# Delta-rule output read out with tokens on partitions, the root of the mean square applied at the residual

## The reference

```python
# log_alpha <= 0 per key channel, Gg its running sum within a chunk; M lower triangular, from keys, decays, beta
u = solve_triangular(M, vg - kexp @ S)                 # unit diagonal
o = SCALE * ((qg * exp(Gg)) @ S + attn @ u)            # attn: decayed products of query and keys
S = exp(glast) * S + kdec.T @ u
...
rstd = rsqrt(mean(square(o), axis=-1) + NORM_EPS)      # over the 128 value channels
o = o * rstd * onorm_w * sigmoid(gate)
x = x + o.reshape(b, t, H * DV) @ Wo.T
```

## Time and profile before

| | us |
|---|---|
| median of three runs | 5018.0 |
| span of the profiled execution | 5005.7 |
| VectorE busy | 4134.4 (83%) |
| ScalarE busy | 3484.7 (70%) |
| GpSimd busy | 3217.8 (64%) |
| mean of 60 periods, 428.26 to 4621.15 | 69.88 |

### The profile page before, as it was taken

The page is one execution under the profiler, slowest core; times in us unless marked ns, Lnnn a source line. Parts: engine busy times, 40 slices in busy tenths (PEclk is TensorE's granted clock), DMA queues, the critical chain, the costliest instruction groups (busy, mean ns, idle before and its releaser), DMA issues.

```text
span 5005.7 us, 151432 instructions
## 1 busy us (share of the span) xinstructions
PE 4517.9 (90%) x63200; PEld 3131.9 (63%) x63200; DVE 4134.4 (83%) x7262; ACT 3484.7 (70%) x6775; POOL 3217.8 (64%) x5316
## 2 busy tenths in 40 slices
PE   8869999999999999999999999899999999999888
PEld 5536666666666666666666666666666666666655
DVE  3289998888988899889998899888998899988622
ACT  3367777777777777777777777777777777777531
POOL 0047777776777777777777777777777777777600
PEclk9979999999999999999999999999999999999899
DMA  2200000000000000000100000000000000000100
GB/s 88 94 21 21 25 25 25 16 22 25 34 32 15 28 25 25 25 14 25 34 32 28 15 25 25 25 16 23 30 29 25 14 24 25 25 25 8 38 9 21
DMA packets 49724, 135.45 MB, mean 27 GB/s; under 512 B 7056, under 2 KB 28176, under 8 KB 48400
## 3 DMA queue, kind: packets, MB, share of 16 engines
q1 hardware_dynamic: 49040, 125.77, 7.2%
HBM read 111.60 MB, written 14.16 MB: 25 GB/s over the span
## 4 chain that ended last, share of the span: by engine, by line
PE 54%; DVE 26%; ACT 11%; issue 7%; POOL 1%; DMA 0%; DVEq 0%; SPq 0%; ACTq 0%
PE bank L835 46%; DVE acc L1557 8%; PE bank L302 7%; DVE X L1554 7%; DVE sp_t L1554 2%; ACT L1432 2%; DVE Pd L1662 2%; ACT Us L1181 2%; ACT o L1182 1%; DVE Zc L1741 1%; DVE Rs L1557 1%; DVE o L1557 1%; ACT acc L1181 1%; PE bank L906 1%; DVE x1m L1554 1%
## 5 line engine op out<-in xcount | busy, mean ns | idle before, releaser
L1557 DVE SCALAR_TENSOR_TENSOR acc<-bank,vc,acc 128x510 f32<-128x510 f32 (+2 forms) x1728 | 1272.9, 740 | 148.5 <-ACT acc L1181 122.9
L2002 POOL TENSOR_TENSOR LZ<-LZ,LT 128x120 f32<-128x120 f32 (+26 forms) x1984 | 957.3, 483 | 155.5
L1999 POOL TENSOR_TENSOR LT<-LA,LZ 128x120 f32<-128x120 f32 (+26 forms) x1984 | 917.1, 462 | 145.9
L1554 DVE TENSOR_TENSOR X<-KQ,Fl 128x640 f32<-128x640 f32 x1024 | 1002.8, 995 | 1.5 <-ACT Fl L1182 1.5
L1972 POOL COPY X<-KQ 128x640 f32<-128x640 f32 x256 | 246.4, 962 | 912.4 <-PE bank L835 312.2
L835 PE MATMUL bank<-X 128*32 128x60 f32 (+1 forms) x32768 | 650.8, 205 | 132.6 <-DVE Pd L1662 85.9
L835 PEld LDWEIGHTS bank<-X 128*32 128x32 f32 x32768 | 524.7, 112 | 369.1 <-issue 211.0
L1181 ACT ACTIVATE Us<-bank 128x128 f32<-128x128 f32 x1024 | 281.2, 276 | 621.3 <-PE bank L835 615.2
L835 PE MATMUL bank<-xnTm,WK 128*128 128x512 f32 x1280 | 662.7, 643 | 42.0 <-DVE acc L1557 36.3
L835 PE MATMUL bank<-Rs,Ztf 128*128 128x128 f32 x2048 | 467.4, 314 | 68.8 <-DVE Rs L1557 48.6
L1951 POOL TENSOR_TENSOR kdec<-KQ,Fe 128x512 f32<-128x512 f32 x256 | 336.8, 1316 | 299.4 <-PE bank L906 299.4
(11 more groups left out here) (145 smaller groups left out, 9346.4 us busy)
## 6 DMA issues: line engine op xcount, KB each, us to landing
WK<-in_wkq SPq DMA_DIRECT2D x64, 704.0 KB, 5.9
WV<-in_wv SPq DMA_DIRECT2D x64, 576.0 KB, 3.8
WO<-in_wo SPq DMA_DIRECT2D x64, 128.0 KB, 2.0
wuh<-in_wu SPq DMA_DIRECT2D x2, 1024.0 KB, 7.4
xt<-in_x SPq DMA_DIRECT2D x4, 512.0 KB, 6.2
wuh_d<-wuh SPq DMA_DIRECT2D x1, 2048.0 KB, 6.3
x_d<-x SPq DMA_DIRECT2D x4, 512.0 KB, 3.1
xnT_d<-xT SPq DMA_DIRECT2D x4, 512.0 KB, 2.7
```

The source lines that it names most:

```text
L1554: return e.tensor_tensor(o, a, b, op)
L1557: return e.scalar_tensor_tensor(out=o, in0=a, scalar=sc, in1=b, op0=op0, op1=op1)
L1999: e.tensor_tensor(tmp, LA[:, j + 1:32, 8 * (j % R) + j // R].unsqueeze(2).broadcast_to([P, rr, cc]), LZ[:, j, 0:cc].unsqueeze(1).broadcast ...
L2002: e.tensor_tensor(LZ[:, j + 1:32, 0:cc], LZ[:, j + 1:32, 0:cc], tmp, SUB).then_inc(g_row, 1)
```

## The change

Four things are changed together.

1. The output is computed with tokens on partitions. `update` keeps only the product for S (chunk 7 has none). A new `attend(s, j)`, j = 0 to 3, computes the outputs of chunks 2j and 2j + 1 of both sequences: At and qn are now the weights (32 columns) and Us and S move (128 columns); each chunk writes 32 partitions of bank 7. Us and S get four buffers per sequence. attend(0) stands behind update(1, 1), attend(1) behind update(1, 4), attend(2) behind update(1, 6), attend(3) behind project_k(p, 4), which goes ahead of it.
2. The mean square is a sum along the free axis: ScalarE copies bank 7 to o2, and squares bank 7 in four parts with `accum_out`, onto itself. Ln and Exp work on four columns (`rstd`). The matmul with ones is gone. `keep(p-1, 0)` goes ahead of the squares.
3. TensorE turns o2 back by four transposes (`turn_o`, behind products(p-1, 1, 0)); VectorE multiplies by the gate alone; the weight onorm_w is multiplied into WO on GpSimd (`weigh_out`); `rstd` is applied where VectorE adds to x1, in four parts. A block of tokens on partitions is 64 tokens of each sequence, so x1 is loaded and stored by two DMAs each.
4. LB and x1 have one buffer each.

The order in bank_use becomes ... v 1, k 3, k 4, oturn 0, out 0, out 1, gate 0 ... .

```diff
-            ("ms", 0, 3, a_ms, 3, 0), ("k", 4, 0, v_ck, 15, 14), ("out", 0, 3, v_out, 2, 0),
-            ("out", 1, 3, v_out, 2, 1), ("gate", 0, 1, a_gate, 1, 0), ("vturn", 0, 2, a_vt, 4, 0),
+            ("k", 4, 0, v_ck, 15, 14), ("oturn", 0, 3, v_o, 1, 0), ("out", 0, 3, v_out, 4, 1),
+            ("out", 1, 3, v_out, 4, 3), ("gate", 0, 1, a_gate, 1, 0), ("vturn", 0, 2, a_vt, 4, 0),
...
 TensorE
-                if c < 7:
-                    mm(bank[5 + hb][:, 2 * P:3 * P], kdT[:, s % 2, u, :], Us[:, hb, :]).then_inc(p_upd, 1)
-                o = bank[7][:, 32 * u:32 * u + 32]
-                ins = mm(o, Us[:, hb, :], At[:, s % 2, u, :], True, c == 0)
-                if c:
-                    ins = mm(o, S[:, hb, c % 2, :], qn[:, s % 2, 32 * u:32 * u + 32], False, True)
+                mm(bank[5 + hb][:, 2 * P:3 * P], kdT[:, s % 2, 8 * hb + c, :], Us[:, hb, c % 4, :]).then_inc(p_upd, 1)
+
+            def attend(s, j):
+                w.wait_ge(a_ssq, every(s - 1, 4))
+                w.wait_ge(a_Us, nth(s, 16, 4 * j + 3))
+                chunks = [(hb, c) for hb in range(2) for c in (2 * j, 2 * j + 1)]
+                for hb, c in chunks:
+                    o = bank[7][half(2 * hb + c % 2), P * j:P * j + P]
+                    ins = mm(o, At[:, s % 2, 8 * hb + c, :], Us[:, hb, c % 4, :], True, c == 0)
+                for hb, c in chunks:
+                    o = bank[7][half(2 * hb + c % 2), P * j:P * j + P]
+                    u = 8 * hb + c
+                    if c:
+                        ins = mm(o, qn[:, s % 2, 32 * u:32 * u + 32], S[:, hb, c % 4, :], False, True)
                 ins.then_inc(p_o, 1)
...
-            def mean_square(s):
-                o = bank_for("ms", 0, s)
-                w.wait_ge(a_osq, every(s, 1))
-                mm(o[:, :], ones, o2[:, :]).then_inc(p_ms, 1)
+            def turn_o(s):
+                o = bank_for("oturn", 0, s)
+                w.wait_ge(a_o, every(s, 1))
+                for j in range(4):
+                    ins = e.transpose(o[:, P * j:P * j + P], o2[:, P * j:P * j + P], ident)
+                ins.then_inc(p_ot, 1)
...
                 solve(p - 3, 1, 7)
                 spare(p - 3, 22)
-                update(p - 3, 0, 7)
-                update(p - 3, 1, 7)
+                project_k(p, 4)
+                attend(p - 3, 3)
                 spare(p - 3, 23)
-                mean_square(p - 3)
-                project_k(p, 4)
                 products(p - 1, 1, 0)
+                turn_o(p - 3)
 ScalarE
                 w.wait_ge(p_sol, nth(s, 16, 2 * c + hb))
-                act(Us[:, hb, :], bank[5 + hb][:, P:2 * P], ACT.Copy).then_inc(a_Us, 1)
+                w.wait_ge(p_o, nth(s - 1, 4, c // 2 + 2) if c < 4 else nth(s, 4, c // 2 - 2))
+                act(Us[:, hb, c % 4, :], bank[5 + hb][:, P:2 * P], ACT.Copy).then_inc(a_Us, 1)
...
-                act(o2[:, :], bank[7][:, :], ACT.Square, scale=SCALE).then_inc(a_osq, 1)
+                act(o2[:, :], bank[7][:, :], ACT.Copy).then_inc(a_o, 1)
+            def out_square(s, j):
+                o = bank[7][:, P * j:P * j + P]
+                e.activation(o, o, ACT.Square, scale=SCALE, accum_out=ssq[:, j:j + 1]).then_inc(a_ssq, 1)
...
-                out_square(p - 3)
+                out_copy(p - 3)
                 e.preload_act_table_set("natural_log_exp_and_others")
                 decay(p, 2)
+                keep(p - 1, 0)
+                out_square(p - 3, 0)
...
                 out_root(p - 3, 0)
                 out_root(p - 3, 1)
-                keep(p - 1, 0)
                 tap_k(p, 4)
 VectorE
-                    stt(o2[:, :], sg[:, s % 2, :], 1.0, o2[:, :], ADD, MUL).then_inc(v_o, 1)
-                    stt(o2[:, :], bank[7][:, :], hon[:, 0:1], o2[:, :], MUL, MUL).then_inc(v_o, 1)
+                for b in range(2):
+                    ins = stt(ov[:, b], gv[:, b], 1.0, tv[:, b], ADD, MUL)
...
-                tt(xv, bank[bank_use["out", q, s][0]][:, :], xv, ADD).then_inc(v_out, 1)
+                b = bank[bank_use["out", j // 2, s][0]][:, D * (j % 2):D * (j % 2) + D]
+                stt(x1[:, j, :], b, rstd[:, j:j + 1], x1[:, j, :], MUL, ADD).then_inc(v_out, 1)
...
                 evacuate(p - 1, 1, 0)
                 output(p - 3, 0)
+                output(p - 3, 1)
                 evacuate(p - 1, 1, 1)
                 evacuate(p - 1, 1, 2)
-                output(p - 3, 1)
+                output(p - 3, 2)
+                output(p - 3, 3)
                 evacuate(p - 1, 1, 3)
 GpSimd, behind level(p - 1, 2)
+                e.tensor_scalar(WO[:, s % 2, :], WO[:, s % 2, :], hon[:, 0:1], None, MUL).then_inc(g_wo, 1)
 SyncE
-                w.wait_ge(g_row, every((n - 1) * H - 1, 62))
+                w.wait_ge(v_Cn, every(n * H - 1, 2))
...
-                w.wait_ge(d_x2[n % 2], 16 * (n // 2))
-                e.dma_start(x1[:, n % 2], by_tile(x1_d)[n]).then_inc(d_x1[n % 2], 16)
+                if n:
+                    w.wait_ge(d_x2[(n - 1) % 2], 32 * ((n + 1) // 2))
+                for hb in range(2):
+                    e.dma_start(x1[64 * hb:64 * hb + 64], by_chunk(x1_d)[n, hb]).then_inc(d_x1, 16)
```

More of the change, by code:

```diff
@@ L660, in build @@
         onw = vc[:, H * 39:H * 39 + 1]
[L661 removed]
+        x1 = sb("x1m", [P, 4, D])
         tctx.close()
@@ L674, in build @@
         p_inv = [sem(f"p_inv{i}") for i in range(4)]
-        p_rhs, p_sol, p_upd, p_o, p_ms, p_out = (sem(f"p_{n}") for n in ("rhs", "sol", "upd", "o", "ms", "out"))
+        p_rhs, p_sol, p_upd, p_o, p_ot, p_out = (sem(f"p_{n}") for n in ("rhs", "sol", "upd", "o", "ot", "out"))
         a_tapk, a_tapv, a_k, a_v, a_gate, a_decay = (sem(f"a_{n}") for n in ("tapk", "tapv", "k", "v", "gate", "decay"))
@@ L686, in build @@
         v_Rs, v_S, v_o, v_out = (sem(f"v_{n}") for n in ("Rs", "S", "o", "out"))
-        g_zero, g_kdec, g_kexp, g_copy, g_X0, g_init, g_row = (sem(f"g_{n}") for n in ("zero", "kdec", "kexp", "copy", "X0", "init", "row"))
+        g_zero, g_kdec, g_kexp, g_copy, g_X0, g_init, g_row, g_wo = (sem(f"g_{n}") for n in ("zero", "kdec", "kexp", "copy", "X0", "init", "row", "wo"))
         def turns(order, count):
@@ L791, in delta_sync @@
                     if h == H - 1:
[L792 to L795, removed]
+                        store_x1(n)
+                        if n + 1 < NT:
+                            load_x1(n + 1)
                 s = p - 1
@@ L1068, in delta_tensor @@
                 update(p - 3, 1, 4)
+                attend(p - 3, 1)
                 spare(p - 3, 14)
@@ L1086, in delta_tensor @@
                 update(p - 3, 1, 6)
+                attend(p - 3, 2)
                 spare(p - 3, 20)
@@ L1159, in delta_tensor @@
                 update(p - 2, 1, 1)
+                attend(p - 2, 0)
                 spare(p - 2, 5)
@@ L1324, in turned @@
                 if q == 0:
-                    w.wait_ge(p_o, every(s - 2, 16))
+                    w.wait_ge(p_upd, every(s - 2, 14))
                 act(kdT[:, s % 2, 4 * q:4 * q + 4, :].rearrange("p n d -> p (n d)"),
@@ L1332, in keep @@
                 w.wait_ge(p_prod, nth(s, 20, 5 * b + 4))
-                w.wait_ge(p_o, every(s - 2, 16))
+                w.wait_ge(p_o, every(s - 2, 4))
                 w.wait_ge(v_bd, every(s - 2, 1))
@@ L1345, in place @@
                 w.wait_ge(v_Ztc, every(s, 1))
-                w.wait_ge(p_o, every(s - 1, 16))
+                w.wait_ge(p_sol, every(s - 1, 16))
                 act(Ztf[q, :, q], Ztc[q, :, :], ACT.Copy).then_inc(a_Ztf, 1)
@@ L1960, in spread @@
                 else:
-                    w.wait_ge(p_o, every(s - 2, 16))
+                    w.wait_ge(p_rhs, every(s - 2, 14))
                     scaled(kexp[:, s % 2, 4 * q:4 * q + 4], Fe[:, 0, :]).then_inc(g_kexp, 1)
```

112 lines of the change are left out of this document (66 added, 46 removed).

## The result

The changed kernel takes 5299.4 us (median of four runs, 5296.75 to 5301.17) where the kernel before took 5016.3 in the same comparison: a ratio of 1.056, with a 95% interval of 1.0539 to 1.0577. The direction was as forecast (0.75 for slower), the size was not: +283 us where +116 was forecast, outside the range of 4985 to 5210.

The account below looks back on a forecast made before the run. No engine bounds the whole: VectorE bounds unfold to beta step, recurrence and read-out are chains between engines. Read-out +3.6 us less recurrence gain 1.7 gives +1.9 a period, 115 us in 60: 5134 us, range 4985 to 5210.

Parts of the forecast that it names:

- The read-out chain: From TensorE's last chunk to the unfold: project_k(p, 4) ahead and ScalarE's later copy lengthen it by 3.6 us a period.
- TensorE's wait (near 3 us): Sign of being right: TensorE's wait behind the last attend is its longest, near 3 us, put down to ScalarE's E.
- output(0) waiting for acc: Sign of being right, in the read-out: output(0) waits for VectorE's acc, since it uses the bank of key block 4.
- How much of the 3.0 arrives? ... Taken: 1.7: Recurrence: of TensorE's 3.0 us of saved work a period, 1.7 shortens the path; bounds 0.8 and 3.0.
- shrinks by 1.2 to 2: Sign of being right: the time from beta step to last convolution of v shrinks by 1.2 to 2 us.
- I leave the clock's cost ... as it is: Clock term, whole period: its cost stays 0.94 us a period, despite a longer stand-still of 3.1 us.
- a fall in every period, twice: Rival: clock falls in two stretches every period, costing 2.7 us for 0.94: 5238 us; 0.15 for beyond the forecast.
- part of the slow work lies in slack: Argument against the clock rival: some work at the lower clock lies in slack; no size given.
- Buffers 0: Single buffers for beta and x1: three changes of tile at 0 us each, 5 at most.
- The tiling rule as a rival: Rival, recurrence: TensorE's saving wins, read-out keeps its length, 1.77 us a period gained, 4912 us; chance 0.17.

Follow-up runs that it names:

- e2: Changed kernel plus 14 unused TensorE matmuls behind attend(3), filling its 3.3 us wait: 5216.4 us, ratio 1.040 to the kernel before.
- e6: Changed kernel with e5's read-out order, and attend(0), (1), (2) moved to where TensorE waits anyway: 4906.0 us, ratio 0.978 to the kernel before.
- e5: Changed kernel with read-out reordered: attend(3), turn_o, project_k(p, 4); banks in that order; ScalarE's block 4 tap before squares and roots: 4998.7 us, ratio 0.9967 to before.
- e8: Kernel before plus unused fill matmuls, three ahead of mean_square and two behind it: 5032.4 us, ratio 1.004.
- e4: Kernel before with one buffer each for beta and x1, nothing else of the change: 5019.8 us against 5022.4, ratio 1.0004.
- e7: Changed kernel with only its three early attend groups moved to e6's places, read-out unchanged: 5275.5 us, ratio 1.051 to the kernel before.
- e10: Changed kernel with attend(0), (1), (2) cut to one matmul each, other outputs of chunks 0 to 5 left out: 5274.0 us, ratio 1.051 to before.

## Why the prediction was right in direction and wrong in size

**The read-out chain: right, 0.5 us short.** Counted from the start of `project_k(p, 4)`, forecast against e2 at full clock and against after:

| us from project_k(p, 4) | forecast | e2, full clock | after |
|---|---|---|---|
| copy of o | 2.4 | 2.6 | 2.6 |
| tap of block 4 | 7.1 | 7.4 | 7.4 |
| gating | 6.7 | 7.1 | 8.0 |
| output(0) | 10.1 | 10.5 | 11.1 |
| unfold | 13.4 | 13.95 | 14.9 |

Squares and roots took 1.26 and 0.44 (2530.46 to 2531.72 to 2532.16) for 1.1 and 0.5; the attend group 0.58 for 0.5 to 0.6; no table was reloaded; the gating's two halves took 0.67 start to start. What was stated of TensorE's wait (near 3 us) and of output(0) waiting for acc shows in both traces. Term: +4.1 against before's 9.87, +3.6 forecast; 0.5 x 60, 29 us unrounded.

**"How much of the 3.0 arrives? ... Taken: 1.7": the step that failed first.** It was 0.4: conv_v(1, 0) ends 31.42 us behind the beta step, 31.81 before. The work did go (TensorE busy 22.99 us between the beta step and the third value projection, 24.83 before), and the time did not (26.28 against 26.69): waits took its place. Of the signs that the prediction named for being right, this one failed ("shrinks by 1.2 to 2"). I followed the handovers with the work removed, and charged the added groups to TensorE's total, not to the place where each one stands. Each stands between the update and the next solve, where the next chunk is waiting for TensorE (at 2518.76 it holds up S x kexp until 2519.34), and gives back 0.58 of what the dropped pairs had gained. At e6's places the same projection starts 1.2 us earlier, and before's is beaten by 1.6, which is near the 1.7 that I took. So the size was there to be had, at other places. e6 moves the three groups together; what each one costs where it stood was not measured. Missing: 1.31 x 60 = 79 us.

**"I leave the clock's cost ... as it is": the step that failed second.** The clock shows 0.93 in 49 of 61 first parts and 0.96 in the others, never 1.00, where before shows 1.00 in 42. In the period shown it falls near the end of the wait of 3.31: the clock is 1.00 up to 2529.50 and 0.50 from 2530.50, and products, turned o and output stand on the chain there (1.0 us between e2's column and after's). It falls again behind the next wait, of 1.50, at 2555.42: from 2556.00 on 0.58, though TensorE is busy for 7.47 of these 7.50 us, and the part takes 29.49 where at full clock it takes 27.25. This second fall comes in 36 of 61 periods (6 before), and the same wait, 1.43 to 1.50 us, stands in those where it doesn't come, and before; what decides is not shown. The sum for a period is 75.0 - 69.9 less 3.7 for the order, 1.4 us, or 85 us in 60; e2, which fills the first wait, gets 83 back, and with 0.978 it also has before's mean clock. I had this as a rival (a fall in every period, twice: 5238, within a chance of 0.15): the clock's cost would grow from 0.94 to 2.7 a period. It grew to 2.3 (74.96 - 45.36 - 27.25), so the rival held nearly in full and should have been in the sum. Its "part of the slow work lies in slack" held too: nearly half of the 14.92 us is at half the clock and lengthens them by 1.0 only.

Together 29 + 79 + 85 - 14 (outside the 60 periods, 13 less where 1 more was forecast) = 179, of a miss of 177 in the spans (293.5 less 116). That the sum closes proves little, since the clock's term is what the others leave of the period; e2's 83 us is its check.

The Trainium skill (TensorE: Matmul & The Clock Gate, HAM oscillation) tells of a kernel whose TensorE drops to the lower rate in each tile, since its wait recurs in each. The rows of the first parts agree: the wait of 3.31 and a clock below 1.00 stand in all 61. One of its cures there is to reorder the loop; here e5 does that, and 41 of 61 first parts are at 1.00. e8 shows that filling a wait is no sure substitute.

**The rest: right.** Buffers 0 (e4: 1.0004). The tiling rule as a rival, that TensorE's saving wins, was wrong for the change as made, and e6 shows it right for the same work in another order: 4906 us, where that rival had 4912. The agreement is partly luck: the period shrinks by 1.21 us (69.85 to 68.64), 73 us in 60, not by the 1.77 of that rival. Of the 98 us between the two spans, 16 lie in the drain behind the last beta step (260.2 against 276.4), where I did not look.

## What to carry to other kernels

Price an added instruction at the place where it stands, by what waits for the engine right there, and not in the engine's sum: here one exchange of two lines was worth 206 us, and the placement of three groups 93 us, with the same work (24 us while the read-out was out of order). When an edit makes a long wait on TensorE in every period, price the work behind it at the lower clock as well, and count the periods at each clock, in each part, before a difference of some 20 us is put down to an order: in e7, e8 and e10 the second part gave back more than half of what the first had gained; and before giving up a rewrite that came out slower, try its pieces in the order in which their users wait.

## What the runs showed of the hardware, not expected

- A small group of column-tiled matmuls costs more than its matmuls add: one matmul (two records) takes 0.34 us to the start of the next full-width matmul, and the whole group of eight (16 records) 0.58, of which the first four take 0.24 (2526.71 to 2526.95). The first group, with 12 records, takes no less, 0.57. A full-width matmul holds TensorE for 0.22 to 0.33 in the same stretch. What part is the change from one tiling to the other was not measured by itself.
- A square with its sum at the side is two instructions, an ACTIVATE of 0.28 and an ACTIVATION_READ_ACCUMULATOR of 0.19, and one such pair follows the other after 0.28 us (2530.46, 2530.74).
- Filling a wait can move the fall of the clock elsewhere: e8 has a full clock in the read-out in 60 of 61 periods, and a lower one in the second part in 21, before in 6. It needn't: with e2's fills the second part shows 0.88 in 3 periods, after in 26.
- A fall of the clock in the second part costs twice in e8: that part takes 28.8 and not 27.25, and the first part behind it 42.7 and not 41.68.
- TensorE was busy for 3.33 of 3.50 and for 7.47 of 7.50 us in the two stretches at the lower clock: a high busy share in the rows goes with the lower clock there, since the same matmuls last longer (the products 1.02 us against 0.63).
